# An fp32 matmul of four rows run over all 128 rows, its added weight rows zero

## The chip, the cores and the metric

One NeuronCore of a Trainium2 chip runs the whole program in one launch. The metric is device time in microseconds (us) of that launch.

## The reference, cut to what matters

Sixteen graphs of 512 nodes with 128 features go through four graph layers, each with a layer norm ahead and a residual behind. The change lies in the fourth layer (layer3 in the kernel). Its part that matters:

```python
s = x @ w_se.T + b_se                       # 512 nodes x 3 coordinates
sq = jnp.sum(s * s, axis=-1)
dist = sq[:, :, None] + sq[:, None, :] - 2.0 * jnp.einsum('bnd,bmd->bnm', s, s)
A = jnp.exp(-dist) * mask
msg = jax.nn.relu(x @ w_msg.T + b_msg)
x_nmp = jnp.einsum('bnm,bmd->bnd', A, msg)
```

Beside it the layer has a convolution over 17 taps along the nodes, and a gated cell (two sigmoids and a tanh) that takes both results. The other layers are an attention of 8 heads (layer0), an attention with one score matrix (layer1), and five rounds of message passing with a gated cell (layer2).

## The kernel before

Everything of a graph is held transposed, features on the 128 partitions and 512 nodes along the row, so one matmul has 512 columns and fills one PSUM bank. Graphs alternate between two slots `s` (g % 2), each with its own buffers and its own four PSUM banks `B[s]`. Each engine's program is made of strands (for TensorE: weights, values, keys, heads, layer1, layer2, layer3, taps), each a generator for one graph. `in_order` merges the strands of all graphs by a table of times, `START` per graph and `TURN` per step, so work of one graph's heads stands among another's layer3 and taps. That order is fixed when the program is built; on the chip, semaphores alone hold an instruction back.

A product that needs fp32 accuracy is mostly done as three fp32r matmuls (`mm3`, lines 506, 507 and 510: high weights times high data, low weights times high data, high weights times low data). Some are plain fp32: the transposes (a matmul with the identity, such as lines 636, 797, 563, 570), the attention products of line 642, the weighted sum of line 821, and line 801. In the trace a plain fp32 matmul of 512 columns has two MATMUL records and two LDWEIGHTS records; the view names its shape as weight rows * weight columns, then the moving operand.

The distance of layer3 is made with one matmul per tile of 128 nodes (line 811) from an augmented operand of `AUG` = 101 rows: four blocks at rows 0, 32, 64 and 96, each of five rows (three coordinates, and two rows for the squared norm and for the constant 1). That operand comes about like this, for each graph:

1. `mm3` with the weights `se` (line 793) puts the three coordinates, without bias, four times into bank 2 of `B[s]`, rows 0 to 100.
2. ScalarE squares rows 0 to 3 of the bank with the bias added (line 1018) and writes them to rows 0 to 3 of `F[s][:, 2, :]`. The fourth row of the bank is zero and its bias 1, so that row is 1. Semaphore `sq3`.
3. TensorE transposes `msg` (line 797, four transposes of 128x128), then waits for `sq3` and runs line 801: weights `cols[0:4, nq0:nq0+101]` times `F[s][0:4, 2, :]`, added into the same bank. The weights are -1 at the norm rows and the bias at the coordinate rows. Semaphore `aug_banked`.
4. ScalarE (line 1026) and VectorE (line 1415) split the bank into its high and low parts; then line 811 follows.

The weights `nq` are built on the host as a 128 x 101 array that is zero from row 4 on, and are loaded once with `cols`:

```python
nq, pick = _np.zeros((P, AUG), _np.float32), ...
for b in range(BLOCKS):
    nq[0:3, 32 * b + 3:32 * b + 5] = -1.0
    nq[3, 32 * b:32 * b + 3] = v["L3_gnn_b_se"]
```

`F[s]` has eight such slices of 128 x 512. Slice 2 is also written in full, all 128 rows, by layer1 (line 958) and by the gates of the cells (`gate_act`, line 971), so rows 4 to 127 hold numbers of the same graph's last layer2 cell when line 801 runs.

Behind line 801 TensorE goes on with the taps of the convolution (`high` and `low` with `C1`, lines 506, 507 and 510). A later place that the prediction speaks of is the turn from one graph to the next: the cell's result `Y[s]` (in the buffer accY, written at line 1366) is transposed back at line 570, VectorE adds it to X (line 1169), and a matmul of the next graph's values (line 506, weights and data exchanged) waits for that. Ahead of that wait stand 16 filling matmuls (`busy`, line 556).

Of the kernel before, what the change touches and what calls it, by code (L numbers as in the profile page):

```python
# [35 lines left out]
BLOCKS, ROWS5 = 4, 5  # L36
AUG = 32 * (BLOCKS - 1) + ROWS5
# [6 lines left out]
CI = {n: i for i, n in enumerate(COLS)}  # L44
# [130 lines left out]
def build(nc, x, adj, adjt, nmask, c2w, wraw, prew, fcw, fpw, cols_d, out):  # L175
    with ExitStack() as ctx:
        def sb(name, shape, dt=F32):
            return ctx.enter_context(nc.sbuf_tensor(name, shape, dt))
# [14 lines left out]
        cols = sb("cols", [P, len(COLS)])  # L193
# [16 lines left out]
        F = [sb(f"F{s}", [P, 8, NODES]) for s in SL]  # L210
# [34 lines left out]
        B = [ctx.enter_context(nc.psum_tensor(f"banks{s}", [P, 4, 512], F32)) for s in SL]  # L245
# [32 lines left out]
        def after(name, turn, k=None):  # L278

            return S[name], turn * PER[name] + (PER[name] if k is None else k)  # L280

        def own(name, g, turn):

            return OS[name][g % SLOTS], (g // SLOTS) * OWN[name] + turn + 1
# [23 lines left out]
        def part(t):  # L308
            return slice(t * P, (t + 1) * P)
# [188 lines left out]
        def _(pe):  # L498
            def mm3(dst, w, xs, start=True, stop=True):

                high(dst, w, xs, start)
                return low(dst, w, xs, stop)

            def high(dst, w, xs, start=True):

                pe.matmul(dst, w[0], xs[0], start=start, stop=False)  # L506
                pe.matmul(dst, w[1], xs[0], start=False, stop=False)  # L507

            def low(dst, w, xs, stop=True):
                return pe.matmul(dst, w[0], xs[1], start=False, stop=stop)  # L510

            def W(name, j=0, n=DIM):
                a = WCOL[name] + j * DIM
                return WH[:, a:a + n], WLO[:, a:a + n]
# [39 lines left out]
            def busy(bank, n):  # L554
                for k in range(n):
                    pe.matmul(bank, WH[:, 0:P], WH[:, 0:4 * P])  # L556

            def transpose_in(g, turn):

                s = g % SLOTS  # L560
                for t in range(TILES):
                    pe.wait_ge(*own("normed", g, turn * TILES + t))
                    last = pe.transpose(B[s][:, 0, part(t)], hN[s][:, part(t)], ident[:, :])  # L563
                last.then_inc(OS["h_banked"][s], 1)

            def transpose_out(g, y):

                s = g % SLOTS
                for t in range(TILES):
                    last = pe.transpose(B[s][:, 1, part(t)], y[:, part(t)], ident[:, :])  # L570
                last.then_inc(OS["y_banked"][s], 1)
# [200 lines left out]
            def layer3(g):  # L772
                s = g % SLOTS
                cell = g * (LAYERS2 + 1) + LAYERS2
                yield
                if g == GRAPHS - 1:
                    pe.wait_ge(*after("r", cell - 1))
                    busy(B[s][:, 2, :], 10)
                pe.wait_ge(*after("h_new", cell - 1))
                transpose_out(g, HT[s])  # L780
                yield
                if g == GRAPHS - 1:
                    busy(B[s][:, 2, :], 13)
                transpose_in(g, 3)
                yield
                pe.wait_ge(*own("h_high", g, 3))
                high(B[s][:, 1, :], W("c1"), (HH[s], HL[s]))
                high(B[s][:, 3, :], W("msg"), (HH[s], HL[s]))
                pe.wait_ge(*own("h_low", g, 3))
                low(B[s][:, 1, :], W("c1"), (HH[s], HL[s])).then_inc(S["c1_banked"], 1)  # L790
                low(B[s][:, 3, :], W("msg"), (HH[s], HL[s])).then_inc(S["msgt_banked"], 1)
                yield
                mm3(B[s][0:AUG, 2, :], W("se", 0, AUG), (HH[s], HL[s])).then_inc(S["s3_banked"], 1)
                yield
                pe.wait_ge(*after("msgt", g))
                for t in range(TILES):
                    last = pe.transpose(B[s][:, 1, part(t)], F[s][:, 5, part(t)], ident[:, :])
                last.then_inc(S["msg_banked"], 1)
                yield
                pe.wait_ge(*after("sq3", g))  # L800
                pe.matmul(B[s][0:AUG, 2, :], cols[0:ROWS5 - 1, CI["nq0"]:CI["nq0"] + AUG], F[s][0:ROWS5 - 1, 2, :],
                          start=False, stop=True, skip_group_check=True).then_inc(S["aug_banked"], 1)
                for t in range(TILES):
                    yield
                    if t == 0:
                        pe.wait_ge(*after("aug", g))
                    elif t == 1:
                        pe.wait_ge(*after("msg", g))
                    else:
                        pe.wait_ge(*after("dist_exped", g, t - 1))  # L810
                    pe.matmul(B[s][:, t % 2, :], R[s][0:AUG, 1, part(t)], R[s][0:AUG, 0, :])\
                        .then_inc(S["dist_banked"], 1)
                yield
                h, c, n = (HH[s], HL[s]), (R[s][:, 0, :], R[s][:, 1, :]), (R[s][:, 2, :], R[s][:, 3, :])
                pe.wait_ge(*after("dist_exped", g))
                mm3(B[s][:, 0, :], W("hh3", 0), h, stop=False)
                mm3(B[s][:, 1, :], W("hh3", 1), h, stop=False)
                for t in range(TILES):
                    yield
                    pe.wait_ge(*after("weights3", g, t + 1))  # L820
                    last = pe.matmul(B[s][:, 2, :], F[s][:, 7, part(t)], PT[s][:, t, :], start=(t == 0),  # L821
                                     stop=(t == TILES - 1))
                last.then_inc(S["nmp_banked"], 1)
                yield
                if g == GRAPHS - 1:
                    pe.wait_ge(*after("c2_scaled", g))
                    busy(B[s][:, 3, :], 13)
                pe.wait_ge(*after("nmp_low", g))
                mm3(B[s][:, 0, :], W("ih3n", 0), n, start=False, stop=False)
                mm3(B[s][:, 2, :], W("ih3n", 2), n, stop=False)  # L830
                mm3(B[s][:, 1, :], W("ih3n", 1), n, start=False, stop=False)
                yield
                pe.wait_ge(*after("c2_scaled", g))
                mm3(B[s][:, 3, :], W("hh3", 2), h).then_inc(S["hn_banked"], 1)
                yield
                pe.wait_ge(*after("xc_high", g))
                high(B[s][:, 0, :], W("ih3c", 0), c, start=False)
                high(B[s][:, 2, :], W("ih3c", 2), c, start=False)
                yield
                pe.wait_ge(*after("xc_low", g))  # L840
                low(B[s][:, 0, :], W("ih3c", 0), c).then_inc(S["r_banked"], 1)
                low(B[s][:, 2, :], W("ih3c", 2), c).then_inc(S["in_banked"], 1)
                yield
                mm3(B[s][:, 1, :], W("ih3c", 1), c, start=False).then_inc(S["z_banked"], 1)
                yield
                pe.wait_ge(*after("h_new", cell))
                transpose_out(g, Y[s])

            def taps(g):
# [15 lines left out]
                last.then_inc(S["c2_banked"], 1)  # L865

            in_order("PE", weights, values, keys, heads, layer1, layer2, layer3, taps)


# [647 lines left out]
```

## Time and profile before

| | |
|---|---|
| median of three runs | 2161.02 us (2158.74 to 2164.31) |
| the profiled execution, its own time | 2156.58 us |
| its span in the trace | 2154.8 us |
| TensorE busy (matmul) | 2077.1 us, 96% |
| VectorE, ScalarE, GpSimd busy | 1617.7, 1503.3 and 772.6 us |
| mean granted TensorE clock | 0.994 |

How to read it: PE is TensorE's matmuls, PEld its weight loads, which have a record of their own and can run under an earlier matmul; DVE is VectorE, ACT ScalarE, POOL GpSimd. A matmul's end is modelled from its shape, so what is read is the distance from one start to the next. The clock is a share of 2.4 GHz: 1.00 is 2.4 GHz, 0.50 is 1.2 GHz.

### The profile page before, as it was taken

Reading aid. Unit: us, or ns where it says so; the run is one execution under the profiler, and the core shown is the slowest. Engines: PE = TensorE matmul, PEld = TensorE weight load, DVE = VectorE, ACT = ScalarE, POOL = GpSimd, SP = SyncE. Lnnn points to the kernel's source line nnn. Section 1 sums busy time; section 2 is a strip of 40 time slices with the busy share of each in tenths; the row PEclk is TensorE's granted clock in tenths of the full one; section 3 lists DMA queues with packets and bytes.
Section 4 is the critical chain, followed back from the end, with each engine's and each line's share of the span. In section 5 each row is a group of like instructions: output and inputs, shape, how many; then the busy total and the mean of one; then the engine's idle time right before and its main releaser. Section 6 shows DMA issues by size and latency. Waiting matters only on the chain. (4 is left out here: it accounts for less than half of the span.)

```text
span 2154.8 us, 34486 instructions
## 1 busy us (share of the span) xinstructions
PE 2077.1 (96%) x12526; PEld 1758.3 (82%) x12526; DVE 1617.7 (75%) x4801; ACT 1503.3 (70%) x2984; POOL 772.6 (36%) x888
## 2 busy tenths in 40 slices
PE   6899999999999999999999999999999999999987
PEld 6778797887978878797887978878797887979865
DVE  6687887868778677887868778687887868778653
ACT  6677594967849577594967849577694967859532
POOL 2433334243423424344243423434333343423411
PEclk9999999999999999999999999999999999999999
DMA  3101000010100101001010100101000010100100
GB/s 126 45 21 45 25 14 32 25 45 25 45 25 1 45 25 45 25 6 40 26 45 25 45 25 1 45 25 45 25 30 22 20 45 25 45 6 1 45 6 5
DMA packets 47306, 65.61 MB, mean 30 GB/s; under 512 B 3744, under 2 KB 21536, under 8 KB 47008
## 3 DMA queue, kind: packets, MB, share of 16 engines
q1 hardware_dynamic: 47136, 63.42, 8.9%
q8 instruction: 98, 1.61, 0.3%
q14 instruction: 72, 0.59, 0.1%
HBM read 59.22 MB, written 4.19 MB: 29 GB/s over the span
## 5 line engine op out<-in xcount | busy, mean ns | idle before, releaser
L642 PE MATMUL banks<-F,PT 128*128 128x128 f32 x4096 | 543.8, 276 | 3.1 <-ACT PT L936 2.4
L642 PEld LDWEIGHTS banks<-F,PT 128*128 128x128 f32 x4096 | 509.0, 192 | 18.8 <-DVE PT L1238 4.7
L443 POOL TENSOR_SCALAR U<-U,rden 128x512 f32<-128x512 f32 x192 | 132.5, 698 | 297.2 <-DVE rden L1230 297.2
L1238 DVE COPY PT<-banks 128x512 f32<-128x512 f32 x256 | 175.2, 684 | 77.6 <-PE banks L636 75.3
L971 ACT ACTIVATE F<-banks,dcols 128x512 f32<-128x512 f32 x288 | 195.7, 686 | 49.5 <-PE banks L510 45.6
L936 ACT ACTIVATE PT<-banks 128x512 f32<-128x512 f32 x256 | 151.2, 591 | 85.4 <-PE banks L636 85.4
L443 POOL TENSOR_SCALAR tiles<-tiles,rden 128x512 f32<-128x512 f32 x192 | 137.5, 727 | 134.8 <-DVE rden L1230 134.6
L476 POOL TENSOR_TENSOR HS<-HT,HS 128x512 fp32r<-128x512 f32 x64 | 83.5, 1304 | 240.1 <-ACT HS L1000 240.1
L443 POOL TENSOR_SCALAR adjT<-adjT,rden 128x512 f32<-128x512 f32 x128 | 88.6, 696 | 194.6 <-DVE rden L1230 194.5
L506 PE MATMUL banks<-HS,WH 128*128 128x512 f32 (+1 forms) x368 | 153.0, 416 | 1.5 <-ACT HS L899 1.4
L413 POOL TENSOR_TENSOR rstd<-var,mhalf 128x4 f32<-128x4 f32 x64 | 67.0, 1047 | 240.4 <-DVE var L1138 240.4
L507 PE MATMUL banks<-HS,WLO 128*128 128x512 f32 (+1 forms) x368 | 145.5, 395 | 0.0
L926 ACT ACTIVATE tiles<-tiles 128x512 f32<-128x512 f32 x192 | 138.5, 721 | 0.7
L926 ACT ACTIVATE U<-U 128x512 f32<-128x512 f32 x192 | 137.7, 717 | 1.7
L922 ACT ACTIVATE tiles<-tiles,QN 128x513 f32<-128x513 f32 x192 | 138.1, 719 | 0.1
L922 ACT ACTIVATE U<-U,QN 128x513 f32<-128x513 f32 x192 | 136.7, 712 | 0.1
L510 PE MATMUL banks<-R,WH 128*128 128x512 f32 x336 | 135.4, 411 | 0.0
L506 PE MATMUL banks<-R,WH 128*128 128x512 f32 x336 | 133.9, 399 | 0.0
L507 PE MATMUL banks<-R,WLO 128*128 128x512 f32 x336 | 132.6, 395 | 0.0
L1220 DVE CUSTOM_DVE_ANT_0 U<-adjN,banks 128x512 f32<-128x512 f32 x192 | 126.9, 680 | 0.0
L510 PE MATMUL banks<-HS,WH 128*128 128x512 f32 (+1 forms) x368 | 126.6, 394 | 0.0
L1220 DVE CUSTOM_DVE_ANT_0 tiles<-adjN,banks 128x512 f32<-128x512 f32 x192 | 125.5, 680 | 1.0 <-issue 1.0
(221 smaller groups left out, 5352.0 us busy)
## 6 DMA issues: line engine op xcount, KB each, us to landing
adjN<-in_adj_dram SPq DMA_DIRECT2D x32, 1024.0 KB, 5.6
adjT<-in_adjt_dram SPq DMA_DIRECT2D x16, 1024.0 KB, 5.5
xin<-in_x_dram SPq DMA_DIRECT2D x18, 256.0 KB, 2.8
out_dram<-X SPq DMA_DIRECT2D x16, 256.0 KB, 5.9
F<-in_wraw_dram SPq DMA_DIRECT2D x1, 1076.0 KB, 9.7
adjT<-in_c2w_dram SPq DMA_DIRECT2D x1, 1024.0 KB, 11.7
PT<-in_fcw_dram SPq DMA_DIRECT2D x1, 512.0 KB, 5.7
PT<-in_fpw_dram SPq DMA_DIRECT2D x1, 512.0 KB, 7.1
```

What stands on the lines that cost most here:

```text
L443: pool.tensor_scalar(SC[s][h % RING][:, t, 0:NODES], SC[s][h % RING][:, t, 0:NODES], rden[s][:, h % RING, t:t + 1], 1.0, ALU.mult, ALU.mul ...
L476: pool.tensor_tensor(HL[s], HT[s][:, :], HH[s].bitcast(F32), ALU.subtract).then_inc(S["h_new_low"], 1)
L506: pe.matmul(dst, w[0], xs[0], start=start, stop=False)
L507: pe.matmul(dst, w[1], xs[0], start=False, stop=False)
L510: return pe.matmul(dst, w[0], xs[1], start=False, stop=stop)
L642: last = pe.matmul(B[s][:, 3, part(j)], PT[s][:, k, part(j)], G[s][:, k, h * DIM:(h + 1) * DIM], start=(h == 0 and j == 0 and k == 0), sto ...
L922: act.activation(SC[s][h % RING][:, t, :], SC[s][h % RING][:, t, :], ACT.Prelu, bias=QN[s][:, t, h:h + 1], scale=0.01, alpha=100.0).then_i ...
L926: act.activation(SC[s][h % RING][:, t, 0:NODES], SC[s][h % RING][:, t, 0:NODES], ACT.Exp, bias=SC[s][h % RING][:, t, NODES:NODES + 1], sca ...
L936: act.activation(PT[s][:, j, :], pt_bank(s, j), ACT.Copy).then_inc(S["pt_act"], 1)
L971: act.activation(F[s][:, tile, :], B[s][:, bank, :], func, bias=dcol(bias), scale=0.5)\
L1220: dve.tensor_tensor_reduce(out=SC[s][h % RING][:, t, 0:NODES], in0=adjN[s][:, t, :], in1=B[s][:, 0, :], scale=1.0, scalar=3.0e38, op0=ALU. ...
L1238: dve.tensor_copy(PT[s][:, j, :], pt_bank(s, j)).then_inc(S["pt_dve"], 1)
```

## The change

Line 801 uses all 128 rows of the weights and of the moving operand. The added weight rows are the zero rows of `nq`; the added rows of the moving operand are rows 4 to 127 of slice 2 of `F[s]`. The result is the same sum. No other line differs, and each engine's sequence of instructions and waits is the same as before.

```diff
                 pe.wait_ge(*after("sq3", g))
-                pe.matmul(B[s][0:AUG, 2, :], cols[0:ROWS5 - 1, CI["nq0"]:CI["nq0"] + AUG], F[s][0:ROWS5 - 1, 2, :],
+                pe.matmul(B[s][0:AUG, 2, :], cols[:, CI["nq0"]:CI["nq0"] + AUG], F[s][:, 2, :],
                           start=False, stop=True, skip_group_check=True).then_inc(S["aug_banked"], 1)
```

## Rows read from the trace of the kernel before

**Rows 1.** The page: busy time per engine, and granted clock in 40 slices.

```profile
PE 2077.1 (96%) x12526; PEld 1758.3 (82%) x12526; DVE 1617.7 (75%) x4801; ACT 1503.3 (70%) x2984; POOL 772.6 (36%) x888
...
PEclk9999999999999999999999999999999999999999
```

**Rows 2.** Waits of TensorE, 264 to 1984: total us, times, longest us.

```profile
PE banks L506 <- DVE X L1169: 23.8, 13, 4.0
PE banks L730 <- DVE HT L1366: 4.2, 13, 0.3
PE banks L570 <- DVE accY L1366: 3.6, 13, 0.3
```

**Rows 3.** Timeline of TensorE's matmuls around line 801: start, us, what, count.

```profile
338.55 0.60 PE L797 MATMUL banks<-ident,F 128*128 128x128 f32 x4
339.08 1.10 PE L801 MATMUL banks<-F,cols 4*101 4x512 f32 x2
340.11 0.51 PE L506 MATMUL banks<-C,WH 128*128 128x512 f32 x1
340.45 0.40 PE L507 MATMUL banks<-C,WLO 128*128 128x512 f32 x1
340.68 0.40 PE L506 MATMUL banks<-C,WH 128*128 128x512 f32 x1
```

**Rows 4.** The same view, four transposes and what follows them.

```profile
206.09 0.60 PE L636 MATMUL banks<-ident,tiles 128*128 128x128 f32 x4
206.53 1.06 PE L642 MATMUL banks<-F,PT 128*128 128x128 f32 x8
```

**Rows 5.** The same view, fp32 matmuls of 128 rows and 512 columns.

```profile
355.22 1.88 PE L821 MATMUL banks<-PT,F 128*128 128x512 f32 x4
356.94 0.60 PE L696 MATMUL banks<-ident,F 128*128 128x128 f32 x4
357.29 0.48 PE L668 MATMUL banks<-R 128*128 128x512 f32 x1
357.61 0.40 PE L671 MATMUL banks<-R 128*128 128x512 f32 x1
```

**Rows 6.** The second record of line 801, by itself.

```profile
339.59 0.59 PE L801 MATMUL banks<-F,cols 4*101 4x512 f32 x1
```

**Rows 7.** Timeline, weight loads and matmuls of line 821.

```profile
353.20 0.43 PEld L821 LDWEIGHTS banks<-PT,F 128*128 128x128 f32 x2
353.43 1.02 PE L821 MATMUL banks<-PT,F 128*128 128x512 f32 x2
```

**Rows 8.** Timeline of weight loads around line 801, in brackets the loader's idle time.

```profile
339.08 0.25 PEld L801 LDWEIGHTS banks<-F,cols 4*101 4x101 f32 x2 [0.17 <-issue]
340.11 0.19 PEld L506 LDWEIGHTS banks<-C,WH 128*128 128x128 f32 x1 [0.78 <-issue]
```

**Rows 9.** Timeline of TensorE, line 811 among other matmuls.

```profile
475.45 0.42 PE L811 MATMUL banks<-R 101*128 101x512 f32 x1
475.70 0.39 PE L510 MATMUL banks<-C,WH 128*128 128x512 f32 x1
```

**Rows 10.** The chain that ended last, in the last graph.

```profile
2123.36 1.03 PE banks L801 x2
```

**Rows 11.** Windows: stretch, its length, busy us per engine, then granted clock, DMA share, GB/s.

```profile
246.84:250.24 3.40, 3.40 (x12) 2.81 (x13) 2.09 (x9) 0.69 (x2) 0.00 (x0) 0.50 0.55 95
...
1666.79:1670.19 3.40, 3.40 (x12) 2.83 (x12) 2.03 (x10) 0.60 (x1) 0.00 (x0) 0.50 0.60 120
505.40:509.40 4.00, 4.00 (x23) 3.19 (x24) 3.96 (x12) 1.40 (x3) 0.00 (x0) 1.00 0.31 43
```

**Rows 12.** Timeline of TensorE, the wait for X.

```profile
245.76 0.50 PE L506 MATMUL banks<-WH,HS 128*128 128x512 f32 x1 [1.63 <-DVE X L1169]
```

**Rows 13.** Timeline of TensorE, line 801 in the next graphs.

```profile
468.96 1.10 PE L801 MATMUL banks<-F,cols 4*101 4x512 f32 x2
597.40 1.10 PE L801 MATMUL banks<-F,cols 4*101 4x512 f32 x2
```

## The prediction

> **What bounds the kernel now.** I read the page first. TensorE is busy 96% of the span, VectorE 75%, ScalarE 70%, and the granted clock is 9 tenths or more in every slice [rows 1]. So the next question is how much TensorE waits once the kernel is in its steady state. The view of waits over the stretch 264 to 1984 us, about 13 graphs, gives three kinds only: 23.8 us for X of line 1169, 4.2 us for HT and 3.6 us for accY of line 1366 [rows 2]. That is 31.6 us, about 2.4 us a graph out of a period of 128.5 to 130 us. All three are ends of chains that begin with a matmul. Between the changed instruction and the next accY, in the stretch 209 to 238, the view of TensorE's waits is empty. TensorE's own time is therefore the bound, and a TensorE time taken away in each graph should shorten each graph by the same.
>
> **The instruction before.** Line 801 is one fp32 matmul per graph; the trace shows it as two records with two weight loads. Durations of matmuls are modelled and overlap, so I count from start to start.
>
> One graph, record by record [rows 3]: four transposes of line 797 begin at 338.55, line 801 begins at 339.08, the next matmul (line 506 of the taps) at 340.11, and the one behind that (line 507) at 340.45. From the first transpose to line 507 that is 1.90 us.
>
> The same sequence with all rows is not in the trace, but each of its pieces is:
> - Four transposes: 206.09 to 206.53, 0.44 us [rows 4]. In front of line 801 they take 0.53 us. Extra: 0.09 us.
> - Two records of a full-height fp32 matmul with 512 columns: four of line 821 run from 355.22 to the next kind at 356.94, 1.72 us, so 0.43 each and 0.86 for two [rows 5]. Line 801 takes 1.03, its second record starting at 339.59, 0.51 behind the first [rows 6]. Extra: 0.17 us.
> - The next fp32r matmul, from its true beginning to its successor, 0.23 us; in the ordinary run of taps the starts stand 0.23 apart (340.45, 340.68) [rows 3]. A first fp32r record behind fp32 ones is shown 0.09 early, as at 357.29 where four transposes from 356.94 end at 357.38 and line 671 follows at 357.61 [rows 5]: so 0.23 is right there too. Behind line 801 it is 340.11 to 340.45, 0.34. Extra: 0.11 us.
>
> The weight loads tell why. Before line 821 the first load starts at 353.20 and the matmul at 353.43: it ran under the matmul ahead [rows 7]. Before line 801 the load starts at 339.08, together with its own matmul, after 0.17 us in which the loader stood idle for nothing that is shown; and the load behind it starts at 340.11, again together with its matmul, after 0.78 us of idleness [rows 8]. The load of line 801 does not run ahead, nor does the one that follows it. My reading is that the array works in another shape for the 4-row matmul, and that what is in it has to end before and after; no row shows the shape. The Trainium skill, TensorEngine Tiling (Array Packing), Key Properties, says that a change of tiling mode drains TensorE; the late loads [rows 8] agree with that for entry and exit, and do not show the mode itself.
>
> **The change part by part.** The count, the order and the waits of all instructions stay as they are, on every engine. What changes is the number of rows: 128 for the weights and for the moving operand, in place of 4.
> - Gain: 1.90 minus (0.44 + 0.86 + 0.23 = 1.53) is 0.37 us a graph. Sixteen graphs: 5.9 us.
> - Bounds of it. Above, the same 5.9 us: no piece can go below its ordinary spacing. Below, nothing (0), if the extra belongs to this fp32 matmul with 101 output rows and not to its 4 input rows; and a small loss, if 101-row shapes cost what line 811's do, which are spaced 0.25 where their neighbours have 0.23 [rows 9]: 0.02 for each of two records, 0.6 us over the kernel. I take the upper end, because the entry and exit parts (0.20 of 0.37) are tied to the late weight loads, and line 821, also fp32, has no late load at its entry [rows 7].
> - Cost of the larger transfer within the instruction: nothing. Line 821 streams 128 rows in the 0.43 used above.
> - Rows 4 to 127 of the moving operand hold an older gate of the same graph, and their weights are zero. The instruction waits for the square on ScalarE, which is younger than those rows and already awaited, so no wait is added.
> - The readers behind it, line 1026 on ScalarE and line 1415 on VectorE, get their bank up to 0.26 us earlier. In the last graph line 801 stands on the chain that ended last with 1.03 us [rows 10], so the gain counts there as well.
>
> The profiled execution took 2156.58 us, its span 2154.8. It stands 4.4 us below the median of the runs, 2161.02. By the sum it would be 2150.7, and the median 2155.1 us, 0.27% faster.
>
> **What can blur this.** Behind the wait for X the granted clock sometimes falls to its lower level, 1.2 GHz (0.50 in the rows): four stretches of this kind stand in the steady state, while the stretch behind another such wait has 1.00 [rows 11]. The engine had idled 1.63 us just before the first of them [rows 12]. Price: line 801 starts at 339.08, 468.96 and 597.40 [rows 3, 13]; the step with a low stretch is 129.88, the one without 128.44. So 1.4 us each. How many of the 14 waits get one differs between executions; the three timed runs lie over 5.6 us, about four stretches. The change moves when each wait falls, so it draws this number anew. I take 2 us as its weight on the median.
>
> **The rivals.**
> 1. *The number of rows is not what costs.* The 0.17 inside, the 0.09 before and the 0.11 behind belong to this fp32 matmul in this place and stay. For it: line 801 is the only one in the kernel with few rows, so no row sets it apart. Against: its late load and the next one [rows 8]. Time: 2161.0 us. Chance 0.17. The Trainium skill, TensorE: Matmul & The Clock Gate, Why this matters for your kernels, gives such a rule: a single matmul with 32 rows takes the time of one with 128. By that rule line 801 gains nothing; no row of this trace tests it.
> 2. *Part of it stays.* Only entry and exit (0.20) go, the two records keep their 0.51 spacing: 16 x 0.20 = 3.2 us, 2157.8 us [rows 6]. Or the gain of each graph turns partly into a longer wait for X, which gives the same. For it: X's chain has steps on VectorE and GpSimd. Against: the chain begins on TensorE and moves with it. Chance 0.20.
> 3. *Slower, by the clock.* The place is the wait for X. If TensorE is early and X is not, the 1.63 us grow to 2.0, and every wait could bring a low stretch: ten more than the profiled execution's four, 10 x 1.4 = 14 us, less 5.9, 2164.7 for the profiled execution and 2169.1 for the median, if its 4.4 us are something else than low stretches. It decides from nine more on (12.6 - 5.9 = 6.7 us); with eight the result is within 0.3%. Chance 0.04.
>
> **How the numbers follow.** A measurement of this kernel can tell about 0.3% from no change: 6.5 us, so below 2154.5 is faster, above 2167.5 slower. The forecast (chance 0.59) is centred at 2155.1 with 2 us on either side: a little over half of it lies within 0.3%, because 5.9 us is just short of 6.5. It gives 0.27 faster, 0.32 same. Rival 1 gives 0.01 faster, 0.15 same, 0.01 slower; rival 2 gives 0.03 faster, 0.17 same; rival 3 slower 0.04. Together 0.31 faster, 0.64 same, 0.05 slower. The range from 2151.0 to 2161.5 leaves out half of rival 1, rival 3 and the low tail.
>
> **What would show it.** In the new profile, right: line 801's two records start 0.43 apart, the transposes ahead of them take 0.44, the first load of line 801 starts before its matmul, and first transpose to line 507 is 1.53; a step between graphs with no low stretch is 128.07 to 128.2; the wait for X stays near 1.65. Wrong in size: the records stay 0.51 apart. Wrong altogether: 1.90 stays. If the wait for X reads 2.0, the gain went there. If the steps are 128.15 and the total has not moved, count the low stretches.

## The result, and the profile after

The changed kernel takes 2153.83 us, the median of six runs (2153.56 to 2155.18). The kernel before, run beside it and before it, takes 2161.55 us (six runs, 2156.61 to 2164.31). The ratio is 0.9967, 95% interval 0.9954 to 0.998: faster by 0.33%, or 7.7 us between the medians, with an interval from 4.3 to 9.9 us. The profiled execution took 2154.16 us with a span of 2152.4, against 2156.58 and 2154.8 before. So the two profiled executions stand only 2.4 us apart.

The timeline of TensorE's matmuls around line 801, to be held against [rows 3] (start us, duration us, engine, what, count):

```profile
337.68 0.60 PE L797 MATMUL banks<-ident,F 128*128 128x128 f32 x4
338.12 1.02 PE L801 MATMUL banks<-F,cols 128*101 128x512 f32 x2
338.57 0.79 PE L506 MATMUL banks<-C,WH 128*128 128x512 f32 x1
339.20 0.40 PE L507 MATMUL banks<-C,WLO 128*128 128x512 f32 x1
```

The second of the two records by itself, against [rows 6]:

```profile
338.55 0.59 PE L801 MATMUL banks<-F,cols 128*101 128x512 f32 x1
```

The weight loads there, against [rows 8]:

```profile
338.01 0.28 PEld L801 LDWEIGHTS banks<-F,cols 128*101 128x101 f32 x2
338.55 0.19 PEld L506 LDWEIGHTS banks<-C,WH 128*128 128x128 f32 x1 [0.26 <-issue]
```

The four transposes take 0.44 us instead of 0.53. The records stand 0.43 apart instead of 0.51. The first load of line 801 starts 0.11 before its matmul instead of together with it. From the first transpose to line 507 it is 337.68 to 339.20, 1.52 us where it was 1.90. The record of line 506 between them is shown at 338.57, 0.02 behind the second record of line 801, which streams until about 338.98 by the spacing of 0.43; so its start is not used, and line 507 closes the sequence in every comparison here. In the last graph the chain that ended last shows the same:

```profile
2121.31 0.86 PE banks L801 x2
```

It is 0.86 us there, where it was 1.03 [rows 10].

TensorE's waits in the stretch 264 to 1984 have not moved from [rows 2] in one digit:

```profile
PE banks L506 <- DVE X L1169: 23.8, 13, 4.0
PE banks L730 <- DVE HT L1366: 4.2, 13, 0.3
PE banks L570 <- DVE accY L1366: 3.6, 13, 0.3
```

So nothing of the gain turned into a longer wait. What did change between these two executions is the clock. The view of windows (stretch, its length, busy us of each engine, granted clock, DMA share, GB/s) shows eight low stretches between 246 and 2000 us, of which three stand here, where the kernel before had four (two of them in [rows 11]):

```profile
246.07:249.47 3.40, 3.40 (x12) 2.81 (x12) 2.15 (x9) 0.83 (x2) 0.00 (x0) 0.50 0.65 108
...
894.61:898.00 3.39, 3.39 (x12) 2.60 (x12) 2.55 (x9) 1.71 (x3) 0.00 (x0) 0.50 0.77 213
...
1795.72:1799.12 3.40, 3.40 (x12) 2.70 (x11) 2.62 (x11) 1.71 (x3) 0.00 (x0) 0.50 0.75 169
```

Line 801 in the first and in the fifteenth graph, and in two graphs between which no such stretch lies:

```profile
208.78 0.59 PE L801 MATMUL banks<-F,cols 128*101 128x512 f32 x1
596.98 0.59 PE L801 MATMUL banks<-F,cols 128*101 128x512 f32 x1
725.13 0.59 PE L801 MATMUL banks<-F,cols 128*101 128x512 f32 x1
2015.48 0.59 PE L801 MATMUL banks<-F,cols 128*101 128x512 f32 x1
```

And the kernel before, in the first and the fifteenth graph:

```profile
209.32 0.67 PE L801 MATMUL banks<-F,cols 4*101 4x512 f32 x1
2016.20 0.67 PE L801 MATMUL banks<-F,cols 4*101 4x512 f32 x1
```

The undisturbed step is 725.13 - 596.98 = 128.15 us; it was 128.43 to 128.6. Yet the fourteen steps together take 1806.70 us after and 1806.88 before. Fourteen times 0.37 is 5.2 us less; four more low stretches at 1.3 us are 5.2 us more. Between the first and the fifteenth graph the profiled executions hide the gain almost whole.

### The profile page after: what moved, and what is told of

Same layout as the page of the kernel before. It is cut to its first block and busy times, and to the rows that moved or that the text cites. A ratio compares the mean times of both kernels' runs of the same rounds, so it can differ in the third digit from the quotient of the medians.

```text
span 2152.4 us, 34486 instructions
## 1 busy us (share of the span) xinstructions
PE 2075.5 (96%) x12526; PEld 1762.2 (82%) x12526; DVE 1618.2 (75%) x4801; ACT 1502.8 (70%) x2984; POOL 771.5 (36%) x888
```

## The experiments

Each kernel ran beside the kernel before on the same chip. The questions were two: what is it in the 4-row matmul that costs 0.37 us, and why do the medians stand 7.7 us apart when the instruction is worth 5.9.

### How many rows

Line 801 of the kernel before with other row counts. The added weight rows are zero.

```diff
-                pe.matmul(B[s][0:AUG, 2, :], cols[0:ROWS5 - 1, CI["nq0"]:CI["nq0"] + AUG], F[s][0:ROWS5 - 1, 2, :],
+                pe.matmul(B[s][0:AUG, 2, :], cols[0:32, CI["nq0"]:CI["nq0"] + AUG], F[s][0:32, 2, :],
```

and the same with 0:64 and 0:96.

> Line 801 with 32 rows instead of 4. Theory (the array works in another shape for few rows, and weight loads then run neither ahead of the matmul nor past it): 32 rows is the same shape as 4, so all stays: first transpose to line 507 takes 1.90 us, the two records start 0.51 apart, first load together with its matmul. Rival (the cost falls with the number of rows in use): a value between 1.90 and 1.52, about 1.81 if it goes with the rows.

> 64 rows. Theory (another shape): half the height is again a shape of its own, so 1.90 us and records 0.51 apart. If only the smallest shape costs: 1.52, records 0.43 apart. Rival (falls with the rows): about 1.71.

> 96 rows. Theory (another shape): three quarters can't be a half or a quarter of the array, so it is worked at full height like line 811 with its 101 rows: 1.52 us to 1.56 us, records 0.43 to 0.45 apart, first load ahead of its matmul. Rival (falls with the rows): about 1.61, between the values of 64 and 128 rows.

The timeline of matmuls with 32 rows:

```profile
339.36 0.60 PE L797 MATMUL banks<-ident,F 128*128 128x128 f32 x4
339.89 1.10 PE L801 MATMUL banks<-F,cols 32*101 32x512 f32 x2
340.92 0.51 PE L506 MATMUL banks<-C,WH 128*128 128x512 f32 x1
341.26 0.40 PE L507 MATMUL banks<-C,WLO 128*128 128x512 f32 x1
```

with 64 rows:

```profile
337.60 0.60 PE L797 MATMUL banks<-ident,F 128*128 128x128 f32 x4
338.13 1.10 PE L801 MATMUL banks<-F,cols 64*101 64x512 f32 x2
...
339.50 0.40 PE L507 MATMUL banks<-C,WLO 128*128 128x512 f32 x1
```

and with 96 rows, and its weight load:

```profile
340.53 0.60 PE L797 MATMUL banks<-ident,F 128*128 128x128 f32 x4
340.97 1.02 PE L801 MATMUL banks<-F,cols 96*101 96x512 f32 x2
...
342.07 0.40 PE L507 MATMUL banks<-C,WLO 128*128 128x512 f32 x1
```

```profile
340.86 0.28 PEld L801 LDWEIGHTS banks<-F,cols 96*101 96x101 f32 x2
```

First transpose to line 507: 1.90 us with 4, 32 and 64 rows, 1.54 with 96, 1.52 with 128. It is a step between 64 and 96 rows, not a slope, so the rival that the cost falls with the rows is out. The changed kernel need not have gone to 128 for it. No row count between 64 and 96 was run, so where the step lies between them is open. Each of the three was timed once, at 2158.81, 2157.18 and 2155.91 us, with 4, 5 and 6 low stretches between 246 and 2000 us, so the plain times say little. Set beside runs of the kernel before at the same mean granted clock they say the same as the timeline: 32 rows took 2158.81 at 0.992, where the kernel before took 2158.83 to 2159.90; 64 rows took 2157.18 at 0.993 against 2157.22 to 2158.45; 96 rows took 2155.91 at 0.990 against 2161.23 to 2163.64.

### What the 0.37 us are made of

First, 4 rows and 128 weight columns (the 27 added output rows are read by nothing):

```diff
-                pe.matmul(B[s][0:AUG, 2, :], cols[0:ROWS5 - 1, CI["nq0"]:CI["nq0"] + AUG], F[s][0:ROWS5 - 1, 2, :],
+                pe.matmul(B[s][:, 2, :], cols[0:ROWS5 - 1, CI["nq0"]:CI["nq0"] + P], F[s][0:ROWS5 - 1, 2, :],
```

> 4 rows as before, but 128 weight columns in place of 101 (the added output rows are not read by anything). It asks what the 0.08 us extra per record is. If it is the weight load, exposed because it can't run under the matmul ahead, it grows with the columns loaded: 0.085 x 128/101 = 0.107, records 0.535 apart, and first transpose to line 507 about 1.95. If it is a fixed pause of the shape: 0.51 and 1.90 stay.

The two records were 0.53 apart (337.33 to 337.86), as the exposed load wants. But the next matmul followed the second record by 0.52 (337.86 to 338.38), just as with 101 columns (339.59 to 340.11). The load costs in one place, not in two. From the first transpose to line 507 it is 1.92 us (336.80 to 338.71, 1.914 to 1.918 over the sixteen graphs): less than the 1.95 that was expected of exposed loads, and more than the 1.90 of a fixed pause. So each of the two was right in part.

```profile
337.86 0.59 PE L801 MATMUL banks<-F,cols 4*128 4x512 f32 x1
```

```profile
336.80 0.60 PE L797 MATMUL banks<-ident,F 128*128 128x128 f32 x4
337.33 1.12 PE L801 MATMUL banks<-F,cols 4*128 4x512 f32 x2
338.38 0.49 PE L506 MATMUL banks<-C,WH 128*128 128x512 f32 x1
338.71 0.40 PE L507 MATMUL banks<-C,WLO 128*128 128x512 f32 x1
```

Second, 4 rows in two matmuls of 256 columns, which makes four records:

```diff
+                for c in (slice(0, 256), slice(256, 512)):
+                    last = pe.matmul(B[s][0:AUG, 2, c], cols[0:ROWS5 - 1, CI["nq0"]:CI["nq0"] + AUG],
+                                     F[s][0:ROWS5 - 1, 2, c], start=False, stop=True, skip_group_check=True)
+                last.then_inc(S["aug_banked"], 1)
```

> Line 801 of the kernel before, 4 rows, as two matmuls of 256 columns each: four records. Theory (entry and exit cost once per change of shape; inside, each record shows its weight load of about 0.085): records 0.213 + 0.085 = 0.30 apart, first transpose to line 507 0.53 + 3 x 0.30 + (0.30 + 0.01) + 0.335 = 2.07 us. Rival (a fixed extra per fp32 matmul, not per weight load): 1.90 + 0.37 = 2.27 us or, if the extra is once only, 1.90.

The matmuls, merged, then the third and the fourth record by themselves:

```profile
336.69 0.60 PE L797 MATMUL banks<-ident,F 128*128 128x128 f32 x4
337.22 1.10 PE L802 MATMUL banks<-F,cols 4*101 4x256 f32 x4
338.25 0.50 PE L506 MATMUL banks<-C,WH 128*128 128x512 f32 x1
338.59 0.39 PE L507 MATMUL banks<-C,WLO 128*128 128x512 f32 x1
```

```profile
337.73 0.37 PE L802 MATMUL banks<-F,cols 4*101 4x256 f32 x1
```

```profile
337.95 0.37 PE L802 MATMUL banks<-F,cols 4*101 4x256 f32 x1
```

The whole is 1.90 us again (336.69 to 338.59), and the theory said 2.07; the value of the rival's second branch, an extra that is there once only, came out. Between the third and the fourth record lie 0.22 us, half of the 0.43 that 512 columns take at full height. So within the 4-row shape later weight loads do run ahead, and I had the middle of the instruction wrong. The loads say the rest:

```profile
337.22 0.16 PEld L802 LDWEIGHTS banks<-F,cols 4*101 4x101 f32 x1 [0.17 <-issue]
```

```profile
337.30 0.16 PEld L802 LDWEIGHTS banks<-F,cols 4*101 4x101 f32 x1
```

```profile
338.25 0.19 PEld L506 LDWEIGHTS banks<-C,WH 128*128 128x128 f32 x1 [0.35 <-issue]
338.36 0.19 PEld L507 LDWEIGHTS banks<-C,WLO 128*128 128x128 f32 x1
```

The fourth record starts at 337.95 and is over after 0.22, at 338.17; the next kind's load starts at 338.25. That is a pause of 0.08 to 0.09, like the 0.53 - 0.44 = 0.09 at the entry. Then each change of shape has one load that nothing covers: the first load of line 801 with 101 columns, whose successor comes 0.08 later (0.02 more with 128 columns), and the first load of line 506 with 128 columns, whose successor comes 0.11 later. Together 0.09 + 0.08 + 0.09 + 0.11 = 0.37 us. The cost belongs to the way into the few-row matmul and the way out of it. It is paid once, whether one 4-row matmul stands between them or two. "Change of shape" is a name for that: the traces show the pauses and the late loads with 64 rows and fewer and their absence with 96 and more, and no view shows the state of the array itself.

### The distance matmul over 128 rows

```diff
-                    pe.matmul(B[s][:, t % 2, :], R[s][0:AUG, 1, part(t)], R[s][0:AUG, 0, :])\
+                    pe.matmul(B[s][:, t % 2, :], R[s][:, 1, part(t)], R[s][:, 0, :])\
```

> The changed kernel, with line 811 (the four distance matmuls of a graph, fp32r, 101 rows) over 128 rows too. Rows 101 to 127 then add leftovers, so the distances are no longer the reference's. It asks whether 101 rows cost anything, as the 0.02 us of line 811 in the bound of the prediction suggests. If yes: its spacing falls from 0.25 to 0.23. If the 0.02 belongs to where the matmul stands: it stays 0.25.

The timeline shows a spacing of 0.25, as in [rows 9]:

```profile
346.04 0.41 PE L811 MATMUL banks<-R 128*128 128x512 f32 x1
346.29 0.40 PE L510 MATMUL banks<-C,WH 128*128 128x512 f32 x1
```

The spacing varies with the place, from 0.23 to 0.27 us. The mean over the 64 matmuls of line 811 is 0.249 us in the kernel before, 0.246 in the changed kernel and 0.247 with 128 rows. So 101 rows cost nothing here that the traces can tell, and the small loss that the prediction used as its lower bound had no ground. The kernel was timed once, at 2159.28 us with ten low stretches between 246 and 2000 us; that time is no evidence on the rows.

### Filling the wait

Between 246 and 2000 us the low stretches come at the wait for X. If TensorE is kept at work there, they should go, and the two kernels can be compared without them.

```diff
-                        busy(B[s][:, 0, :], 16)
+                        busy(B[s][:, 0, :], 22)
```

> The kernel before (4 rows) with 22 instead of 16 filling matmuls ahead of the wait for X (line 597). 6 x 0.23 = 1.4 us of the 1.65 us wait are filled. Theory (the excess of the measured gain over 5.9 us, and the spread of the runs, come from the low stretches of the clock behind that wait): low stretches in the steady state vanish or nearly, the runs lie within 2 us, and the median falls by 1.35 us for each stretch the kernel has, that is 5 to 12 us, to about 2150 to 2156. Rival (the wait itself and nothing about the clock sets the time, the spread has another source): no change within 1 us, or slower if the filling outlasts the wait, and the spread of 5 us stays.

> The changed kernel (128 rows) with 22 filling matmuls. Theory: the difference to the same kernel with 4 rows is now the instruction alone, 16 x 0.37 = 5.9 us, within 1 us, and this is the fastest of the four, about 2144 to 2149. Rival (part of the 7.7 us between the medians is a gain of the rows elsewhere): the difference stays 7 to 8 us. Rival (the low stretches do not depend on this wait): eight stretches stay, and the time is that of the changed kernel, 2154.

With 4 rows: 2154.36 us, the median of eight runs (2150.82 to 2155.33). A ninth, the profiled one, had a granted clock of 0.556 from end to end and took 3482.82 us; with it the median is 2154.9, the figure in the next expectation. The ratio to the kernel before is 0.9966 (0.9951 to 0.9981). With 128 rows: 2146.25 us (2144.14 to 2146.95), ratio 0.9931 (0.9915 to 0.9947). The filling is worth 6 to 8 us to either kernel (0.9966 against 1; 0.9931 against the 0.9967 of the changed kernel, these two from different rounds): matmuls that compute nothing make it faster. The runs do not lie within 2 us as expected, but over 4.5 and 2.8 us. The difference of the two, 8.1 us (8.6 with the ninth run), did not fit the 5.9 that I expected, so I ran the first again for its profile.

> The same kernel as before_fill22 (4 rows, 22 filling matmuls), since its profile came out at a granted clock of 0.556 from end to end and tells nothing of the low stretches. Median measured 2154.9 against 2146.25 of the 128-row kernel with the same filling: 8.6 us, where my theory said 5.9 within 1. Theory A (the instruction is worth 5.9 and the rest is low stretches that the filling left standing in the 4-row kernel): the profile shows 2 to 4 low stretches in the steady state, where the 128-row kernel had one, and the steps without one are 0.37 longer than there. Theory B (the 4-row matmul costs something beyond its own place): steps without a low stretch differ by 0.5 us or more between the two.

It took 2152.73 us (twelve runs, 2150.64 to 2155.16), ratio 0.9969 (0.9958 to 0.998). This time the distance to the 128-row kernel is 6.5 us, so part of the 8.1 was in the runs. Its window behind the wait at 762 us, and that of the 128-row kernel with the same filling:

```profile
761.95:768.70 6.75, 6.75 (x23) 5.57 (x23) 2.64 (x9) 1.71 (x3) 0.00 (x0) 0.50 0.51 173
```

```profile
762.03:765.40 3.37, 3.37 (x12) 2.58 (x11) 1.84 (x6) 1.58 (x3) 0.00 (x0) 0.50 0.60 199
```

This is graph 6, whose wait for X is 4 us long and was filled only in part; one execution had a low stretch of double length there and the other a single one. It is the only place between 246 and 2000 us with a low stretch in either. Theory A holds in part: the filling left low stretches standing, but in one graph and not in several. Theory B does not: the thirteen other steps between the first and the fifteenth graph take 128.52 us in the mean with 4 rows and 128.14 with 128, 0.38 apart. The filling did not shorten those steps, which took 128.43 to 128.6 us without it too; it took the low stretches away and shortened nothing else. So I filled that wait too:

```diff
+                        busy(B[s][:, 0, :], 32 if g == 6 else 22)
```

> The 128-row kernel with 22 filling matmuls, and 32 in the one graph (g = 6) whose wait for X is 4 us instead of 1.65. Theory (a low stretch follows where TensorE idles there): that graph's low stretch goes, 1.35 us less, median about 2144.9, runs within 1.5 us. Rival (that stretch comes from something else): 2146.3 stays, or more, if the ten added matmuls outlast the wait.

It took 2143.84 us (five runs, 2143.14 to 2144.87, a spread of 1.7 us where 1.5 was expected). That is 2.4 us below the one without the extra filling, where 1.35 was expected, but the kernel before was itself 2.7 us lower in these rounds, and the ratio is nearly the same, 0.9929 (0.9911 to 0.9947). The profiles price it: the step over that wait takes 130.41 us where it took 131.71, 1.3 us less, and the low stretch of that graph is gone.

Last, the same filling in both kernels, in the same rounds on the same chip:

> 4 rows, with 22 filling matmuls and 32 in g = 6, as in after_fill22_g6, on the same chip and in the same rounds as its twin with 128 rows. Theory (the instruction alone, 16 x 0.37 = 5.9 us, once the low stretches are gone from both): this kernel's median is 5.9 us, 5.0 to 7.0, above the twin's, near 2149.8, and steps between graphs are 0.37 to 0.40 longer. Rival (the rows are worth more than their place shows, as 7.7 and 8.6 us between medians would have it): 7.5 us or more.

> 128 rows, the twin of before_fill22_g6 and the same kernel as after_fill22_g6. Both theories: about 2143.8, as measured. The difference to the twin decides: 5.9 (5.0 to 7.0) for the instruction alone, 7.5 or more for the rival.

With 4 rows 2150.84 us (nine runs, 2148.76 to 2152.2), with 128 rows 2144.39 us (six runs, 2143.21 to 2145.86). The difference is 6.45 us: inside the 5.0 to 7.0 of the instruction alone, under the 7.5 of the rival. By the times alone the rival is not shut out: drawn anew from these fifteen runs, the difference lies between 4.6 and 7.7 us in 95% of the draws. The steps between graphs speak against it: 128.55 us in the mean with 4 rows and 128.15 with 128, 0.40 apart, where 0.37 to 0.40 was forecast. The profiles place part of the half microsecond above 5.9, as said below; the rest is left open. The wait for X from 264 to 1984 us, in both alike:

```profile
PE banks L506 <- DVE X L1169: 4.0, 13, 0.4
```

It was 23.8 us in total and 4.0 at the longest without the filling. Windows of 5 us behind each of the fourteen waits between 240 and 2000 us all read a granted clock of 1.00; the one of graph 6, 4 rows first:

```profile
762.10:767.10 5.00, 5.00 (x27) 3.88 (x28) 3.05 (x10) 2.39 (x5) 0.00 (x0) 1.00 0.68 237
```

```profile
759.90:764.90 5.00, 4.96 (x27) 3.84 (x27) 3.00 (x10) 2.34 (x5) 0.00 (x0) 1.00 0.72 245
```

Neither has a low stretch from 46 us to the last ones at 2141.4 and 2137.7 us. (One window from 246 to 2100 us would not show it: its mean rounds to 1.00 in the kernel before too, with five low stretches inside.) The view of line 801, first and last start of its 32 records, 4 rows first:

```profile
L801 PE MATMUL banks<-F,cols x32: 587/628/669, 209.3 to 2117.4; 4*101 4x512 f32 x32
```

```profile
L801 PE MATMUL banks<-F,cols x32: 592/592/593, 208.9 to 2111.0; 128*101 128x512 f32 x32
```

From the first record to the last, fifteen graphs on: 1908.1 against 1902.1, 6.0 us less, of which 15 x 0.37 = 5.6 are the instruction. Another 0.6 us lies behind the last line 801, 31.5 us to the end against 30.9; there the clock is low for the last 7.0 us of the one execution and for the last 3.7 of the other.

All profiles together tie the low stretches to the length of the wait. In the eight without added filling, the 4 us wait of graph 6 has one each time, and the waits of about 1.65 us in 42 of 104 cases. In the five with it (the execution at 0.556 left out), none of the 68 waits of 0.3 to 0.4 us has one.

Against the kernel before, the kernel with both fillings has the ratio 0.995 (0.9934 to 0.9967) with 4 rows and 0.9924 (0.9904 to 0.9945) with 128: 0.76% faster. The second interval lies below that of the changed kernel, 0.9954 to 0.998, so it beats both kernels of this document.

## Why the prediction was right

*The bound.* That TensorE's own time is the bound, and that a gain there reaches the end, held. The waits of [rows 2] are unchanged and the steps without a low stretch fell to 128.15, where 128.07 to 128.2 was forecast.

*The sum.* 0.37 us a graph was forecast from 1.90 - 1.53. The profile has 1.52; taken to the nanosecond, 1.889 to 1.899 before and 1.520 to 1.525 after, that is 0.37. Sixteen times 0.37 is 5.9 us; the twins without low stretches are 6.45 apart, and 6.0 from first to last line 801.

*Its parts.* The split was wrong. I had 0.09 before, 0.17 inside and 0.11 behind, and gave rival 2 the case that the 0.17 could stay by itself. Nothing of it belongs to the streaming of the rows: the 0.17 is the first exposed load (0.08) and the pause at the exit (0.09). All four pieces are there with 64 rows and fewer and go together. So the case of rival 2 in which 0.20 goes and 0.17 stays had no ground; the sum was right because it did not use the split. The lower bound by line 811 was wrong too, but nothing was built on it.

*Rival 1, the number of rows does not cost.* Refuted by the step between 64 and 96 rows. The Trainium skill's rule that a matmul with 32 rows takes the time of one with 128 (TensorE: Matmul & The Clock Gate, Why this matters for your kernels) is contradicted here for a matmul between full-height ones: with 32 rows the sequence takes 1.90 us, with 128 it takes 1.52. The Trainium skill's other rule, that a change of tiling mode drains TensorE (TensorEngine Tiling (Array Packing), Key Properties), agrees with the pauses of 0.09 at both ends; no row shows the mode.

*Rival 3, slower by the clock.* The wait for X did not grow: the longest stayed 4.0 and the total 23.8. But the number of low stretches did vary as said, four before and eight after, and the four more took 5.2 us in the profiled execution. Its condition, a longer wait, did not come true; the loss by the clock that it named did come in part, by the number of stretches drawn.

*The time.* 2155.1 was forecast, 2153.83 measured. The 1.8 us by which the medians' difference exceeds 5.9 lie within its interval (4.3 to 9.9). Most of it is the mix of low stretches in the runs: over all comparisons the kernel before ran from 2155.53 to 2168.53 us, and with the waits filled from 2148.76 to 2152.2. The granted clock of each run bears this out. Over 46 runs of the kernel before, the time follows it, from 2156.1 us in the mean at 0.994 to 2166.1 at 0.987. At 0.991, where four of the six runs of the changed kernel stand, the kernel before took 2160.0 in the mean of seven and the changed one 2153.8: 6.2 us apart, near the 5.9. So that the medians came out 7.7 apart owes 1.5 us or so to which runs were drawn. That the change shifts this mix in its own favour, beyond chance, was not shown. Between the likelier outcome within 0.3% (0.64) and faster (0.31), the measured 0.33% came out just on the less likely side, as 0.27% forecast left it close.

## What to carry to other kernels

Among full-height matmuls, a matmul over 64 rows or fewer (4, 32 and 64 were tried) costs two changes of shape: here 0.37 us, as much as 1.6 fp32r matmuls of 512 columns. Where the remaining rows can be made to multiply by zero weights for nothing, give it 96 rows or more; where they can't, put such matmuls one behind another, since two of 4 rows in a row paid the price once. And where TensorE waits for something it can't have earlier, look at the granted clock behind the wait before saying that the idle time costs nothing: filling it was worth more here (10.8 us between the medians with both fillings, 2161.6 to 2150.84) than the change itself (5.9).

## What was not expected of the hardware

- In a row of 4-row matmuls the weight loads run ahead as usual; only the first one does not. I had taken the late loads as a property of each.
- Six more matmuls per graph that compute nothing made the kernel faster by 6 to 8 us. With every wait for X filled, the granted clock was 1.00 throughout from 246 to 2100 us. The nine runs with 4 rows lay within 3.4 us, where fourteen of the kernel before, beside them, lay over 11.4. For the 128-row kernel no such narrowing was shown: its six runs without filling lay within 1.6 us, with both fillings within 2.7.
- One execution ran at a granted clock of 0.556 throughout and took 3482.82 us; it was not seen again with the same kernel, and what caused it stays open. Its page has this line:

```profile
PEclk6555555555555555555555555555555555555555
```
